# State-space loop of a decoder layer: every fourth product of state and C moves from VectorE to GpSimd, reading an SBUF copy of C

## The chip, the cores and the metric

One core of a Trainium2 chip. The metric is the device time of one execution in microseconds (us), and lower is better.

The core has five engines with an instruction queue each: TensorE (PE in the profile; its weight loads are PEld), VectorE (DVE), ScalarE (ACT), GpSimd (POOL) and SyncE (SP). Each runs its own instructions in the order of the program and waits on semaphores for the others. SBUF is the large on-chip memory, PSUM the small one that matmuls write; it has 8 banks of 512 float32 per partition. In this kernel GpSimd is given SBUF tiles alone.

## What is computed

The program is a small decoder of two layers on 1024 tokens of width 128. The change touches only its first part, a state-space block (`mamba`). Cut to what matters:

```python
dt, Bm, Cm = jnp.split(x_dbl, [DT_RANK, DT_RANK + D_STATE], axis=-1)
delta = softplus(dt @ dt_proj_w.T + dt_proj_b)        # 1024 x 256
A = -jnp.exp(A_log)                                   # 256 x 16
def step(s, inp):                                     # over the 1024 tokens
    d_t, B_t, C_t, u_t = inp
    dA = jnp.exp(d_t[..., None] * A)
    dBu = d_t[..., None] * B_t[:, None, :] * u_t[..., None]
    s = s * dA + dBu
    y = jnp.einsum('bds,bs->bd', s, C_t)
    return (s, y)
y = selective_scan(xi, delta, A, Bm, Cm, D)           # sum over 16 states, plus u * D
out = (y * silu(z)) @ out_proj_w.T + x
```

## The kernel before

Channels lie on the 128 partitions (two blocks of them, `c`), tokens on the free axis (1024 columns, two halves `q` of 512). The recurrence over tokens is one scan instruction for each half. So the work is a loop over 32 steps `n`: 2 blocks of channels times 16 states. A step does this:

- **B to SBUF.** TensorE spreads row `n % 16` of B over all partitions with two bf16 matmuls into PSUM banks 0 and 1 (`broadcast(…, 0, b_bcast)`, L386). ScalarE copies it to `b_all` (`copy_b`, L465), which has two slots. GpSimd multiplies it with `du` (delta times the input) into `drive` (L340), a ring of four.
- **Decay.** ScalarE computes exp(delta * A) for each half into PSUM banks 6 and 7 (`decay(n, q)`, L472). Bank 6 is rewritten once the first scan of the step before has read it, bank 7 once the second has.
- **Scan.** VectorE runs `scan(n, 0)` and `scan(n, 1)` (L293) into `state`, two slots; the second takes its initial value from the last column of the first.
- **Product with C.** TensorE spreads C's row over banks 2 and 3 (`broadcast(NS + n % NS, 2, c_bcast)`, the same line L386), and VectorE multiplies `state` with it into `read`, a ring of four (`read_out`, L301).
- **Sum.** TensorE adds `read` to banks 4 and 5 by matmuls with the identity in float32 (`add_state`, L395).

The order on each engine is written out by hand. VectorE: `scan(n, 0)`, `read_out(n-1)`, `scan(n, 1)`. ScalarE in step n: `decay(n, 0)`, `copy_b(n+1)`, `decay(n, 1)`. TensorE in step n: B of n+2 (after `copy_b(n+1)` has read the banks), C of n (after `read_out(n-1)` has read them), `add_state(n-1)`. After 16 steps `gated(0)` adds the skip term (L305) and multiplies by the gate `zs` (L309); `gated(1)` does the same at the end. The output projection and the rest of the layer follow the block.

In the words of the sections below, B(n), C(n) and add(n) are these groups of matmuls on TensorE.

Of the kernel before, what the change touches and what calls it, by code (L numbers as in the profile page):

```python
# [16 lines left out]
ALU = mybir.AluOpType  # L17
ACT = mybir.ActivationFunctionType
# [5 lines left out]
P = 128  # L24
S = 1024
# [4 lines left out]
HALF = 512  # L30
# [90 lines left out]
def mamba(nc, g, t, m):  # L121
# [3 lines left out]
    DI, NS, DR = 2 * D, 16, D // 16  # L125
    NC = DI // P
    TAPS = 4
    ps = g["psum"]
# [30 lines left out]
    du = relu  # L159
# [4 lines left out]
    b_all = m.sb("b_all", [P, 2, S])  # L164
    RING = 4
    drive = m.sb("drive", [P, RING, S])
    state = m.sb("state", [P, 2, S])
    read = m.sb("read", [P, RING, S])
    y = m.sb("y", [P, NC, S])

# [15 lines left out]
    var_ready, root_ready = m.sem("var_ready"), m.sem("root_ready")  # L186
    N_LOADS = 13
    STEPS = NC * NS
    DT0 = BC3

    def wide(b):
        return ps[:, b:b + 2, :].rearrange("p b n -> p (b n)")

    with nc.Block() as block:
        @block.sync
# [24 lines left out]
        def _(dve):  # L220
# [60 lines left out]

            def scan(n, q):
                dve.wait_ge(decay_ready, 2 * n + q + 1)
                if n >= 2:
                    dve.wait_ge(read_ready, n - 1)
                first = slice(q * HALF, (q + 1) * HALF)
                if q == 0:
                    dve.wait_ge(drive_ready, n + 1)
                    before = 0.0
                else:  # L290
                    dve.wait_ge(scanned, 2 * n + 1)
                    before = state[:, n % 2, HALF - 1:HALF]
                dve.tensor_tensor_scan(state[:, n % 2, first], ps[:, 6 + q, :], drive[:, n % RING, first], before,  # L293
                                       ALU.mult, ALU.add).then_inc(scanned, 1)

            def read_out(n):
                dve.wait_ge(scanned, 2 * n + 2)
                dve.wait_ge(c_bcast, n + 1)
                if n >= RING:
                    dve.wait_ge(summed, n - RING + 1)  # L300
                dve.tensor_tensor(read[:, n % RING, :], state[:, n % 2, :], wide(2), ALU.mult).then_inc(read_ready, 1)  # L301

            def gated(c):
                dve.wait_ge(summed, NS * (c + 1))
# [5 lines left out]

            for n in range(STEPS):
                scan(n, 0)
                if n >= 1:
                    read_out(n - 1)
                if n == NS + 1:
                    gated(0)
                scan(n, 1)
            read_out(STEPS - 1)
# [7 lines left out]
        @block.gpsimd  # L326
        def _(pool):
            link = chained(pool, chain["pool"])
            pool.wait_ge(loaded, 16 * N_LOADS)
            w = w_in[:, 0:P].unsqueeze(1).to_broadcast([P, TAPS, P])  # L330
            pool.tensor_tensor(w_tap[:], w, tap_rows[:], ALU.mult).then_inc(taps_ready, 1)
            pool.wait_ge(xn_ready, 1)
            pool.tensor_tensor(g["x"][:], g["x"][:], xn[:], ALU.add).then_inc(x_added, 1)
            for n in range(STEPS):
                c = n // NS
                pool.wait_ge(du_ready, c + 1)
                pool.wait_ge(b_copied, n + 1)
                if n >= RING:
                    pool.wait_ge(scanned, 2 * (n - RING + 1))
                pool.tensor_tensor(drive[:, n % RING, :], du[:, c, :], b_all[:, n % 2, :],  # L340
                                   ALU.mult).then_inc(drive_ready, 1)

        @block.tensor
        def _(pe):
            pe.wait_ge(loaded, 16 * N_LOADS)
            transpose_tiles(pe, h, g["ident"][:], ps, h_ready, hT_psum)
# [36 lines left out]
            def broadcast(row, banks, done):  # L383
                sel = onehot[:, row:row + 1].to_broadcast([BC3, P])
                for n in range(2):
                    last = pe.matmul(ps[:, banks + n, :], sel, split[:, n * HALF:(n + 1) * HALF],  # L386
                                     start=True, stop=True)
                last.then_inc(done, 1)

            def add_state(n):  # L390
                pe.wait_ge(read_ready, n + 1)
# [10 lines left out]
            pe.wait_ge(b_copied, 1)  # L402
            broadcast(1, 0, b_bcast)
            for n in range(STEPS):
                if n + 2 < STEPS:
                    pe.wait_ge(b_copied, n + 2)
                    broadcast((n + 2) % NS, 0, b_bcast)
                if n >= 1:
                    pe.wait_ge(read_ready, n)
                broadcast(NS + n % NS, 2, c_bcast)  # L410
                if n >= 1:
                    add_state(n - 1)
            add_state(STEPS - 1)
            pe.wait_ge(y_ready, NC)
            for i in range(NT):
                for c in range(NC):
# [6 lines left out]
        def _(act):  # L423
# [36 lines left out]

            def copy_b(n):
                act.wait_ge(b_bcast, n + 1)
                if n >= 2:
                    act.wait_ge(drive_ready, n - 1)
                act.activation(b_all[:, n % 2, :], wide(0), ACT.Copy).then_inc(b_copied, 1)  # L465
# [10 lines left out]
            act.wait_ge(relu_ready, NC)  # L476
            for n in range(STEPS):
                decay(n, 0)
                if n + 1 < STEPS:
                    copy_b(n + 1)  # L480
                decay(n, 1)
            act.wait_ge(z_ready, 2)
            act.activation(zs[:, 1, :], zs[:, 1, :], ACT.Silu).then_inc(z_ready, 1)

# [5 lines left out]
NS = 64  # L490
# [2617 lines left out]
```

## Time and profile before

| | |
|---|---|
| time, median of 3 runs | 1830.77 us (1829.9 to 1832.34) |
| the profiled execution: its own time | 1832.86 us |
| the profiled execution: span from first to last instruction | 1831.1 us |
| mean granted clock of TensorE | 0.882 of full speed |
| busy over the span: PE, PEld, DVE, ACT, POOL | 80%, 43%, 72%, 50%, 38% |
| first scan of the loop starts | 50.42 us |
| `gated(1)` ends | 170.61 us |

The state-space loop takes the stretch from about 50 to 171 us of the span; everything else of the program is the same before and after. The shares over the whole span say little about this stretch, so the rows are read from it alone. In a timeline row the first number is the start in the span, the second the duration; `x2` means two instructions merged in one row; the bracket is the time that the engine was idle before, and which instruction released it. Ends of matmuls are modelled, so for TensorE the starts are used.

### The profile page before, as it was taken

The page shows a single profiled execution, that of the slowest core. Times are in us where ns is not written, and L with a number is a line of the kernel's source. Part 1 is how long each engine was busy: PE and PEld are TensorE (multiplying, and loading weights), DVE is VectorE, ACT ScalarE, POOL GpSimd, SP SyncE. Part 2 cuts the span into 40 slices and gives each one's busy share as a digit, 9 for nine tenths or more (in the row PEclk, how much of TensorE's full clock was granted, in tenths as well). Part 3 has the DMA queues.
Part 4 walks back from the last instruction along what each step waited for, and adds up shares of the span by engine and source line. Part 5 has one row for each costly group of instructions (what it writes and reads, how often), then busy time and mean ns, then how long its engine had stood idle before and what let it go on. Part 6 is the DMA issues. An engine that isn't in the chain of part 4 may idle for free. (4 is left out here: it accounts for less than half of the span.)

```text
span 1831.1 us, 19912 instructions
## 1 busy us (share of the span) xinstructions
PE 1457.1 (80%) x6613; PEld 791.4 (43%) x6669; DVE 1319.4 (72%) x3065; ACT 923.9 (50%) x1447; POOL 691.3 (38%) x524
## 2 busy tenths in 40 slices
PE   5776999899985467887888878888857538999798
PEld 2223444355543312544555545555545324333365
DVE  5998568655156479899989999999857465767433
ACT  4654213656312204786777778777831104666321
POOL 0764212122000003888788888878820020000012
PEclk8899999999977768899899999989887757999899
DMA  5000110000057100000000000000020030000000
GB/s 138 1 1 3 46 58 16 0 1 1 0 126 144 47 14 1 1 1 1 1 1 1 1 1 1 1 1 1 1 83 11 15 78 1 1 1 1 1 0 12
DMA packets 30685, 37.21 MB, mean 20 GB/s; under 512 B 13859, under 2 KB 23812, under 8 KB 29448
## 3 DMA queue, kind: packets, MB, share of 16 engines
q1 hardware_dynamic: 29028, 24.03, 4.8%
q10 hardware_dynamic: 1544, 11.79, 3.2%
q8 instruction: 57, 0.93, 0.2%
q14 instruction: 56, 0.46, 0.1%
HBM read 29.57 MB, written 6.24 MB: 20 GB/s over the span
## 5 line engine op out<-in xcount | busy, mean ns | idle before, releaser
L1461 PE MATMUL psum<-film_ka,film_context_qa 97*128 97x512 bf16 (+1 forms) x832 | 343.2, 414 | 143.8 <-DVE search_and_weigh_kept L1656 63.6
L1833 ACT ACTIVATE search_and_weigh_e<-psum,search_and_weigh_bias 128x512 f32<-128x512 f32 (+1 forms) x416 | 267.9, 666 | 110.2 <-PE psum L1463 105.4
L1656 DVE MAX8 search_and_weigh_kept<-psum 128x8 f32<-128x171 f32 (+2 forms) x1216 | 317.3, 323 | 5.0 <-PE psum L1463 3.8
L1463 PE MATMUL psum<-film_kb,film_context_qb 128*128 128x512 bf16 (+1 forms) x777 | 319.1, 411 | 0.0
L1682 DVE SCALAR_TENSOR_TENSOR search_and_weigh_e<-psum,film_context_top,search_and_weigh_e 128x512 f32<-128x512 f32 (+1 forms) x283 | 200.8, 717 | 36.8 <-ACT search_and_weigh_e L1833 34.6
L1704 POOL TENSOR_TENSOR search_and_weigh_e<-search_and_weigh_e,search_and_weigh_keep 128x512 f32<-128x512 f32 (+1 forms) x133 | 150.4, 1131 | 167.3 <-ACT search_and_weigh_keep L1812 163.3
L1461 PEld LDWEIGHTS psum<-film_ka,film_context_qa 97*128 97x128 bf16 x832 | 92.2, 111 | 250.2 <-DVE search_and_weigh_e L1682 95.7
L1738 PEld LDWEIGHTS psum<-ctx_rows,search_and_weigh_mean_T 128*128 128x128 f32 (+1 forms) x816 | 132.3, 208 | 32.8 <-issue 6.0
L1708 POOL TENSOR_TENSOR search_and_weigh_mean<-search_and_weigh_e 128x512 f32<-128x512 f32 (+1 forms) x104 | 133.9, 1288 | 12.7 <-DVE search_and_weigh_e L1682 5.6
L1713 POOL TENSOR_TENSOR search_and_weigh_mean<-search_and_weigh_mean,search_and_weigh_e 128x512 f32<-128x512 f32 (+1 forms) x104 | 127.7, 1227 | 8.2
L1738 PE MATMUL psum<-ctx_rows,search_and_weigh_mean_T 128*128 128x96 f32 (+1 forms) x816 | 129.0, 284 | 0.9
L2912 POOL TENSOR_TENSOR residual<-residual,top_expert_kept 128x1024 f32<-128x1024 f32 x7 | 16.5, 2350 | 295.5 <-DVE top_expert_kept L2869 295.5
L2675 DVE TENSOR_REDUCE gqa_attend_low<-psum 128x1 f32<-128x128 f32 (+7 forms) x128 | 93.9, 754 | 43.4 <-PE psum L2594 41.0
L1712 POOL TENSOR_TENSOR search_and_weigh_e<-search_and_weigh_e 128x512 f32<-128x512 f32 (+1 forms) x91 | 111.6, 1227 | 7.1
L2712 ACT ACTIVATE gqa_attend_prob<-psum 128x512 f32<-128x512 f32 x192 | 84.9, 486 | 51.9 <-PE psum L2607 51.1
L1463 PEld LDWEIGHTS psum<-film_kb,film_context_qb 128*128 128x128 bf16 x832 | 88.5, 106 | 49.9 <-issue 17.4
L985 PE MATMUL psum<-cross_attention_prob,ctx_rows 128*97 128x512 f32 (+1 forms) x204 | 98.1, 603 | 4.6 <-ACT cross_attention_prob L1039 4.6
L340 POOL TENSOR_TENSOR mamba_drive<-mamba_relu,mamba_b_all 128x1024 f32<-128x1024 f32 x32 | 77.2, 2414 | 64.7 <-ACT mamba_b_all L465 31.4
L1039 ACT ACTIVATE cross_attention_prob<-psum 128x1024 f32<-128x1024 f32 (+1 forms) x51 | 51.8, 1019 | 97.1 <-PE psum L998 96.4
L998 PE MATMUL psum<-oss_attention_qc_shifted,ctx_T 97*128 97x512 f32 (+1 forms) x204 | 99.4, 611 | 0.8 <-ACT oss_attention_qc_shifted L1030 0.8
L1811 ACT ACTIVATE search_and_weigh_keep<-search_and_weigh_e,search_and_weigh_below 128x512 bf16<-128x512 f32 (+1 forms) x133 | 93.7, 705 | 0.5
L968 PE MATMUL psum<-ctx_T,cross_attention_qc 97*128 97x512 f32 (+1 forms) x208 | 87.3, 576 | 0.7 <-issue 0.7
(547 smaller groups left out, 2687.5 us busy)
## 6 DMA issues: line engine op xcount, KB each, us to landing
film_kb<-film_k_rows ACTq DMA_DIRECT2D x4, 1601.0 KB
film_ka<-film_k_rows ACTq DMA_DIRECT2D x3, 1601.0 KB
ctx_T<-in_ctx_T SPq DMA_DIRECT2D x1, 2401.5 KB
gqa_experts_w<-in_L_ffn_W SPq DMA_DIRECT2D x1, 2048.0 KB
film_convolve_back<-in_dft_back SPq DMA_DIRECT2D x1, 1728.0 KB, 12.9
film_k_rows<-cross_attention_film_hi SPq DMA_DIRECT2D x6, 256.0 KB, 2.0
film_k_rows<-cross_attention_film_mid SPq DMA_DIRECT2D x6, 256.0 KB, 2.0
film_k_rows<-cross_attention_film_low SPq DMA_DIRECT2D x6, 256.0 KB, 2.0
```

Source lines behind the costliest of these rows:

```text
L985: last = pe.matmul(ps[0:CA, 6 + n, :], ctx[0:rows, k, :], prob[0:rows, k % 3, n * HALF:(n + 1) * HALF], start=k == 0, stop=k == KT - 1)
L998: last = pe.matmul(ps[0:rows, 2 * (k % 2) + n, :], ctx_T[:, k * P:k * P + rows], qc_shifted[:, n * HALF:(n + 1) * HALF], start=True, stop= ...
L1461: pe.matmul(out, a["qa"][0:ROWS, h, rows], a["ka"][0:ROWS, h, c + b:c + b + cols], start=True, stop=False)
L1463: last = pe.matmul(out, a["qb"][:, h, rows], a["kb"][:, h, c + b:c + b + cols], start=False, stop=True)
L1656: last = dve.max(kept[:, h % 2, first + s, :], bank[:, lo:hi])
L1682: dve.scalar_tensor_tensor(out=w, in0=weigh_bank(n, h), scalar=a["top"][:, NH * i + h, TOP - 1:TOP], in1=w, op0=ALU.is_ge, op1=ALU.mult).t ...
L1704: link(pool.tensor_tensor(w[h], w[h], keep[:, k % KEEPS, 0:width], ALU.mult))
L1708: link(pool.tensor_tensor(out, w[0], w[1], ALU.add))
L1712: link(pool.tensor_tensor(w[2], w[2], w[3], ALU.add))
L1713: pool.tensor_tensor(out, out, w[2], ALU.add).then_inc(mean_ready, 1)
L1738: last = pe.matmul(ps[:, 7, 0:DC], mean_T[0:r, n % 2, b:b + P], ctx[0:r, (c + b) // P, 0:DC], start=c + b == 0, stop=c + b + r == S2)
L1833: act.activation(e[:, n % RING, sub, 0:PIECES[u][1]], ps[:, SEARCH_BANKS + q % WEIGH_BANKS, 0:PIECES[u][1]], ACT.Exp, bias=bias[:, i % 2, ...
```

## The change

- `read_out(n)` for n = 1, 5, 9, ..., 29 (8 of 32) is taken from VectorE. GpSimd computes it behind `drive(n+2)`, from `state` and `c_all`, a new SBUF tile that ScalarE fills by `copy_c(n)` behind `decay(n, 1)`.
- TensorE's C of the step after such a product waits for `copy_c` and not for the product.
- `state` gets three slots instead of two, `b_all` three.
- ScalarE copies B two steps ahead: `copy_b(n+2)` stands between `decay(n, 0)` and `decay(n, 1)` where `copy_b(n+1)` stood. TensorE's B of n+2 still stands at the start of its step n, ahead of C of n.
- `add_state` runs two steps behind, and `gated(0)` one step later.

```diff
+    B_RING, STATES = 3, 3
+    b_all = m.sb("b_all", [P, B_RING, S])
+    c_all = m.sb("c_all", [P, S])
...
+    state = m.sb("state", [P, STATES, S])
...
+    POOL_EVERY, POOL_FIRST, POOL_LAG, ADD_LAG = 4, 1, 2, 2
...
+    def read_on_pool(n):
+        return n % POOL_EVERY == POOL_FIRST
...
             for n in range(STEPS):
                 scan(n, 0)
-                if n >= 1:
+                if n >= 1 and not read_on_pool(n - 1):
                     read_out(n - 1)
-                if n == NS + 1:
+                if n == NS + ADD_LAG:
                     gated(0)
                 scan(n, 1)
...
-                pool.tensor_tensor(drive[:, n % RING, :], du[:, c, :], b_all[:, n % 2, :],
+                pool.tensor_tensor(drive[:, n % RING, :], du[:, c, :], b_all[:, n % B_RING, :],
                                    ALU.mult).then_inc(drive_ready, 1)
+                r = n - POOL_LAG
+                if r >= 0 and read_on_pool(r):
+                    pool.wait_ge(scanned, 2 * r + 2)
+                    pool.wait_ge(c_copied, pool_reads(r + 1))
+                    if r >= RING:
+                        pool.wait_ge(summed, r - RING + 1)
+                    pool.tensor_tensor(read[:, r % RING, :], state[:, r % STATES, :], c_all[:],
+                                       ALU.mult).then_inc(pool_read, 1)
...
             for n in range(STEPS):
-                if n + 2 < STEPS:
-                    pe.wait_ge(b_copied, n + 2)
-                    broadcast((n + 2) % NS, 0, b_bcast)
+                if n == 0:
+                    broadcast(NS, 2, c_bcast)
+                if n + B_RING - 1 < STEPS:
+                    pe.wait_ge(b_copied, n + B_RING - 1)
+                    broadcast((n + B_RING - 1) % NS, 0, b_bcast)
                 if n >= 1:
-                    pe.wait_ge(read_ready, n)
-                broadcast(NS + n % NS, 2, c_bcast)
-                if n >= 1:
-                    add_state(n - 1)
-            add_state(STEPS - 1)
+                    if read_on_pool(n - 1):
+                        pe.wait_ge(c_copied, pool_reads(n))
+                    else:
+                        wait_read(pe, n - 1)
+                    broadcast(NS + n % NS, 2, c_bcast)
+                if n >= ADD_LAG:
+                    add_state(n - ADD_LAG)
+            for n in range(STEPS - ADD_LAG, STEPS):
+                add_state(n)
...
+            def copy_c(n):
+                act.wait_ge(c_bcast, n + 1)
+                if n >= POOL_EVERY:
+                    act.wait_ge(pool_read, pool_reads(n))
+                act.activation(c_all[:], wide(2), ACT.Copy).then_inc(c_copied, 1)
...
             for n in range(STEPS):
                 decay(n, 0)
-                if n + 1 < STEPS:
-                    copy_b(n + 1)
+                if n == 0:
+                    copy_b(1)
+                if n >= 1 and n + B_RING - 1 < STEPS:
+                    copy_b(n + B_RING - 1)
                 decay(n, 1)
+                if n == 0:
+                    copy_b(2)
+                if read_on_pool(n):
+                    copy_c(n)
```

How the queues stand. ScalarE from the loop's first copy on, before (L465 is `copy_b`, L472 `decay`):

```order
L465 ACTIVATE mamba_b_all<-psum 128x1024 [waits mamba_b_bcast]
L472 ACT_TABLE_LOAD [waits mamba_delta_ready]
L472 ACTIVATE psum<-mamba_delta,mamba_a_neg 128x512 [waits mamba_relu_ready]
L465 ACTIVATE mamba_b_all<-psum 128x1024 [waits mamba_b_bcast]
L472 ACTIVATE psum<-mamba_delta,mamba_a_neg 128x512 [waits mamba_delta_ready]
L472 ACTIVATE psum<-mamba_delta,mamba_a_neg 128x512 [waits mamba_scanned,mamba_delta_ready]
L465 ACTIVATE mamba_b_all<-psum 128x1024 [waits mamba_drive_ready,mamba_b_bcast]
```

The same place after (L496 is `copy_b`, L509 `decay`, L502 `copy_c`):

```order
L496 ACTIVATE mamba_b_all<-psum 128x1024 [waits mamba_b_bcast]
L509 ACT_TABLE_LOAD [waits mamba_delta_ready]
L509 ACTIVATE psum<-mamba_delta,mamba_a_neg 128x512 [waits mamba_relu_ready]
L496 ACTIVATE mamba_b_all<-psum 128x1024 [waits mamba_b_bcast]
L509 ACTIVATE psum<-mamba_delta,mamba_a_neg 128x512 [waits mamba_delta_ready]
L496 ACTIVATE mamba_b_all<-psum 128x1024 [waits mamba_b_bcast]
L509 ACTIVATE psum<-mamba_delta,mamba_a_neg 128x512 [waits mamba_scanned,mamba_delta_ready]
L496 ACTIVATE mamba_b_all<-psum 128x1024 [waits mamba_drive_ready,mamba_b_bcast]
L509 ACTIVATE psum<-mamba_delta,mamba_a_neg 128x512 [waits mamba_scanned,mamba_delta_ready]
L502 ACTIVATE mamba_c_all<-psum 128x1024 [waits mamba_c_bcast]
L509 ACTIVATE psum<-mamba_delta,mamba_a_neg 128x512 [waits mamba_scanned,mamba_delta_ready]
```

One more copy of B stands ahead of the first decay of step 1, so from there on the copy inside a step is B(n+2) and not B(n+1); and behind the second decay of step 1 stands the copy of C, with the first decay of step 2 behind it.

TensorE in steps 0 and 1, before (L386 with `mamba_b_copied` starts a B group, L386 with `mamba_read_ready` a C group, L395 is `add_state`):

```order
L386 MATMUL psum<-mamba_split,mamba_onehot 128x512 [waits mamba_b_copied]
L386 MATMUL psum<-mamba_split,mamba_onehot 128x512 x3
L386 MATMUL psum<-mamba_split,mamba_onehot 128x512 [waits mamba_b_copied]
L386 MATMUL psum<-mamba_split,mamba_onehot 128x512
L386 MATMUL psum<-mamba_split,mamba_onehot 128x512 [waits mamba_read_ready]
L386 MATMUL psum<-mamba_split,mamba_onehot 128x512
L395 MATMUL psum<-mamba_read,ident 128x512 [waits mamba_read_ready]
L395 MATMUL psum<-mamba_read,ident 128x512
```

TensorE in steps 1 and 2, after (L411 is `broadcast`, L420 `add_state`):

```order
L411 MATMUL psum<-mamba_split,mamba_onehot 128x512 [waits mamba_b_copied]
L411 MATMUL psum<-mamba_split,mamba_onehot 128x512
L411 MATMUL psum<-mamba_split,mamba_onehot 128x512 [waits mamba_read_ready]
L411 MATMUL psum<-mamba_split,mamba_onehot 128x512
L411 MATMUL psum<-mamba_split,mamba_onehot 128x512 [waits mamba_b_copied]
L411 MATMUL psum<-mamba_split,mamba_onehot 128x512
L411 MATMUL psum<-mamba_split,mamba_onehot 128x512 [waits mamba_c_copied]
L411 MATMUL psum<-mamba_split,mamba_onehot 128x512
L420 MATMUL psum<-mamba_read,ident 128x512 [waits mamba_read_ready]
L420 MATMUL psum<-mamba_read,ident 128x512
```

The first sum stands one step later; the order inside a step is B, C, sum as before, and the C of step 2 waits for the copy of C in place of the product.

## Rows read from the trace of the kernel before

**Rows 1.** Busy time by stretch: us, then each engine's busy us (count), PEclk, DMA share.

```profile
64.00:109.00 45.00, 36.15 (x106) 13.99 (x105) 45.00 (x40) 30.34 (x40) 31.60 (x14) 1.00 0.00 1
...
117.40:124.30 6.90, 6.28 (x11) 2.58 (x12) 6.40 (x7) 3.50 (x6) 2.35 (x1) 0.53 0.00 0
```

**Rows 2.** Costliest groups, 64 to 109 us: count, busy us, mean ns, idle before, releaser.

```profile
L472 ACT ACTIVATE psum<-mamba_delta,mamba_a_neg 128x512 f32<-128x512 f32 x27 | 18.7, 692 | 14.6 <-DVE mamba_state L293 14.6
...
L386 PE MATMUL psum<-mamba_split,mamba_onehot 96*128 96x512 bf16 x52 | 15.6, 382 | 8.8 <-DVE mamba_read L301 8.8
```

**Rows 3.** Timeline, 98.8 to 105.8 us: start, duration, engine, line, operation, idle before.

```profile
98.92 1.19 DVE L301 TENSOR_TENSOR mamba_read<-mamba_state,psum 128x1024 f32<-128x1024 f32 x1
...
99.72 1.00 ACT L465 ACTIVATE mamba_b_all<-psum 128x1024 f32<-128x1024 f32 x1
100.04 1.27 DVE L293 TENSOR_TENSOR_SCAN mamba_state<-psum,mamba_state,mamba_drive 128x512 f32<-128x512 f32 x1
...
100.17 0.61 PE L386 MATMUL psum<-mamba_split,mamba_onehot 96*128 96x512 bf16 x2 [0.66 <-DVE mamba_read L301]
...
100.61 1.88 PE L395 MATMUL psum<-mamba_read,ident 128*128 128x512 f32 x4
...
101.23 1.19 DVE L293 TENSOR_TENSOR_SCAN mamba_state<-psum,mamba_drive 128x512 f32<-128x512 f32 x1
101.40 0.69 ACT L472 ACTIVATE psum<-mamba_delta,mamba_a_neg 128x512 f32<-128x512 f32 x1 [0.67 <-DVE mamba_state L293]
...
102.33 0.60 PE L386 MATMUL psum<-mamba_split,mamba_onehot 96*128 96x512 bf16 x2
...
102.51 0.69 ACT L472 ACTIVATE psum<-mamba_delta,mamba_a_neg 128x512 f32<-128x512 f32 x1 [0.42 <-DVE mamba_state L293]
103.14 1.00 ACT L465 ACTIVATE mamba_b_all<-psum 128x1024 f32<-128x1024 f32 x1
103.46 1.27 DVE L293 TENSOR_TENSOR_SCAN mamba_state<-psum,mamba_state,mamba_drive 128x512 f32<-128x512 f32 x1
```

**Rows 4.** Timeline, 44 to 64 us: the first steps of the loop.

```profile
50.42 1.21 DVE L293 TENSOR_TENSOR_SCAN mamba_state<-psum,mamba_drive 128x512 f32<-128x512 f32 x1
...
51.73 1.28 DVE L293 TENSOR_TENSOR_SCAN mamba_state<-psum,mamba_state,mamba_drive 128x512 f32<-128x512 f32 x1
52.35 1.00 ACT L465 ACTIVATE mamba_b_all<-psum 128x1024 f32<-128x1024 f32 x1
...
53.26 0.68 ACT L472 ACTIVATE psum<-mamba_delta,mamba_a_neg 128x512 f32<-128x512 f32 x1
...
54.05 1.20 DVE L301 TENSOR_TENSOR mamba_read<-mamba_state,psum 128x1024 f32<-128x1024 f32 x1
...
56.35 1.20 DVE L293 TENSOR_TENSOR_SCAN mamba_state<-psum,mamba_drive 128x512 f32<-128x512 f32 x1
```

**Rows 5.** Timeline, 44 to 64 us: a copy that waits for TensorE, and step 4's first scan.

```profile
61.88 1.03 PE L386 MATMUL psum<-mamba_split,mamba_onehot 96*128 96x512 bf16 x4
...
62.52 1.02 ACT L465 ACTIVATE mamba_b_all<-psum 128x1024 f32<-128x1024 f32 x1 [0.37 <-PE psum L386]
...
63.58 1.22 DVE L293 TENSOR_TENSOR_SCAN mamba_state<-psum,mamba_drive 128x512 f32<-128x512 f32 x1 [0.30 <-POOL mamba_drive L340]
```

**Rows 6.** Timeline, 100 to 120 us: a GpSimd product and a VectorE product of SBUF tiles.

```profile
111.11 2.34 POOL L340 TENSOR_TENSOR mamba_drive<-mamba_relu,mamba_b_all 128x1024 f32<-128x1024 f32 x1 [1.07 <-ACT mamba_b_all L465]
111.59 2.95 DVE L309 TENSOR_TENSOR mamba_y<-mamba_y,mamba_zs 128x1024 f32<-128x1024 f32 x1
```

**Rows 7.** Timeline, 100 to 120 us: TensorE after a pause.

```profile
118.02 1.03 PE L386 MATMUL psum<-mamba_split,mamba_onehot 96*128 96x512 bf16 x2 [3.92 <-DVE mamba_read L301]
```

**Rows 8.** Timeline, 150 to 180 us: the end of the loop.

```profile
161.23 1.19 DVE L293 TENSOR_TENSOR_SCAN mamba_state<-psum,mamba_drive 128x512 f32<-128x512 f32 x1
...
164.04 3.99 PE L395 MATMUL psum<-mamba_read,ident 128*128 128x512 f32 x8
...
169.38 1.23 DVE L309 TENSOR_TENSOR mamba_y<-mamba_y,mamba_zs 128x1024 f32<-128x1024 f32 x1
```

More of the change, by code:

```diff
@@ L163, in mamba @@
     split = m.sb("split", [BC3, S], BF16)
-    b_all = m.sb("b_all", [P, 2, S])
+    B_RING, STATES = 3, 3
+    b_all = m.sb("b_all", [P, B_RING, S])
+    c_all = m.sb("c_all", [P, S])
     RING = 4
     drive = m.sb("drive", [P, RING, S])
-    state = m.sb("state", [P, 2, S])
+    state = m.sb("state", [P, STATES, S])
     read = m.sb("read", [P, RING, S])
@@ L186, in mamba @@
     var_ready, root_ready = m.sem("var_ready"), m.sem("root_ready")
+    c_copied, pool_read = m.sem("c_copied"), m.sem("pool_read")
     N_LOADS = 13
     STEPS = NC * NS
+    POOL_EVERY, POOL_FIRST, POOL_LAG, ADD_LAG = 4, 1, 2, 2
     DT0 = BC3
@@ L192, in wide, with pool_reads, wait_read @@
         return ps[:, b:b + 2, :].rearrange("p b n -> p (b n)")
+    def read_on_pool(n):
+        return n % POOL_EVERY == POOL_FIRST
+    def pool_reads(n):
+        return sum(read_on_pool(k) for k in range(n))
+    def wait_read(eng, n):
+        if read_on_pool(n):
+            eng.wait_ge(pool_read, pool_reads(n + 1))
+        else:
+            eng.wait_ge(read_ready, n + 1 - pool_reads(n + 1))
     with nc.Block() as block:
@@ L283, in scan @@
                 dve.wait_ge(decay_ready, 2 * n + q + 1)
-                if n >= 2:
-                    dve.wait_ge(read_ready, n - 1)
+                if n >= STATES:
+                    wait_read(dve, n - STATES)
                 first = slice(q * HALF, (q + 1) * HALF)
@@ L291, in scan @@
                     dve.wait_ge(scanned, 2 * n + 1)
-                    before = state[:, n % 2, HALF - 1:HALF]
-                dve.tensor_tensor_scan(state[:, n % 2, first], ps[:, 6 + q, :], drive[:, n % RING, first], before,
+                    before = state[:, n % STATES, HALF - 1:HALF]
+                dve.tensor_tensor_scan(state[:, n % STATES, first], ps[:, 6 + q, :], drive[:, n % RING, first], before,
                                        ALU.mult, ALU.add).then_inc(scanned, 1)
@@ L300, in read_out @@
                     dve.wait_ge(summed, n - RING + 1)
-                dve.tensor_tensor(read[:, n % RING, :], state[:, n % 2, :], wide(2), ALU.mult).then_inc(read_ready, 1)
+                dve.tensor_tensor(read[:, n % RING, :], state[:, n % STATES, :], wide(2), ALU.mult).then_inc(read_ready, 1)
             def gated(c):
@@ L390, in add_state @@
             def add_state(n):
-                pe.wait_ge(read_ready, n + 1)
+                wait_read(pe, n)
                 if n == NS:
@@ L404, in _ @@
             for n in range(STEPS):
-                if n + 2 < STEPS:
-                    pe.wait_ge(b_copied, n + 2)
-                    broadcast((n + 2) % NS, 0, b_bcast)
-                if n >= 1:
-                    pe.wait_ge(read_ready, n)
-                broadcast(NS + n % NS, 2, c_bcast)
-                if n >= 1:
-                    add_state(n - 1)
-            add_state(STEPS - 1)
+                if n == 0:
[3 more added lines that the diff above has]
+                    broadcast((n + B_RING - 1) % NS, 0, b_bcast)
+                if n >= 1:
+                    if read_on_pool(n - 1):
+                        pe.wait_ge(c_copied, pool_reads(n))
+                    else:
+                        wait_read(pe, n - 1)
[4 more added lines that the diff above has]
+                add_state(n)
             pe.wait_ge(y_ready, NC)
@@ L462, in copy_b @@
                 act.wait_ge(b_bcast, n + 1)
-                if n >= 2:
-                    act.wait_ge(drive_ready, n - 1)
-                act.activation(b_all[:, n % 2, :], wide(0), ACT.Copy).then_inc(b_copied, 1)
+                if n >= B_RING:
+                    act.wait_ge(drive_ready, n - B_RING + 1)
+                act.activation(b_all[:, n % B_RING, :], wide(0), ACT.Copy).then_inc(b_copied, 1)
+            def copy_c(n):
[3 more added lines that the diff above has]
+                act.activation(c_all[:], wide(2), ACT.Copy).then_inc(c_copied, 1)
             def decay(n, q):
@@ L478, in _ @@
                 decay(n, 0)
-                if n + 1 < STEPS:
-                    copy_b(n + 1)
+                if n == 0:
+                    copy_b(1)
+                if n >= 1 and n + B_RING - 1 < STEPS:
+                    copy_b(n + B_RING - 1)
                 decay(n, 1)
+                if n == 0:
+                    copy_b(2)
+                if read_on_pool(n):
+                    copy_c(n)
             act.wait_ge(z_ready, 2)
```

## The prediction

> **What bounds the loop now.** I read the stretch of the loop first, because the shares of the whole span say nothing about it. From 64 to 109 us VectorE is busy for 45.00 of 45.00 us, TensorE for 36.15, GpSimd for 31.60, ScalarE for 30.34 [rows 1]. So VectorE's own instructions set the pace. Then the groups: ScalarE's decays were released by VectorE's scans, and TensorE's C waited for VectorE's product [rows 2]. Nobody makes VectorE wait in the steady part. Last the timeline of one step [rows 3]. The reader is to see `scan(15, 0)` at 101.23, the product behind it, `scan(15, 1)` at 103.46; the same second scan of step 14 stands at 100.04. One step takes 3.42 us.
>
> The same rows hold what the change leans on. I name them by step. The product of step 13 ends at 98.92 + 1.19 = 100.11. That releases C(14) at 100.17, then add(13) at 100.61, then B(17) at 102.33. ScalarE runs the first decay of step 16 at 102.51 and `copy_b(17)` at 103.14. A copy can start 0.64 us after its B has started (61.88 to 62.52, where the copy did wait) [rows 5], so B(17) is ready at 102.97. It is 0.17 us early. **The margin between TensorE and ScalarE is 0.17 us of a step of 3.42**, and the whole-span shares hide it.
>
> **The product that goes away.** Between the starts of the two scans of a step lie 2.23 us with a product (101.23 to 103.46) [rows 3] and 1.31 us without one, where the second scan has to wait for the first (50.42 to 51.73) [rows 4]. Eight products less are worth 8 x 0.92 = 7.4 us, if VectorE stays the bound. The Trainium skill (VectorE: DVE Perf Modes, section "The DRAIN you can't avoid") says that a semaphore between VectorE instructions costs nothing extra. By that rule the distance would be 1.12 us and the gain 9.0 us; the trace does not agree, its row shows 1.31 us, so I keep 7.4.
>
> **GpSimd** takes 2.34 us for such a product [rows 6]. Four drives and one product of state and C are 11.7 us in four steps, against 13.7 us that four steps take now. It fits, with less room, and nothing below needs a slower GpSimd.
>
> **The copy of B, one step further ahead.** This is the term that decides. In step 15 ScalarE now wants B(17), not B(16), between its two decays. But TensorE makes B(17) when it did before: at the head of its step 15, behind C(14) and the sum, so ready at 102.97 [rows 3, 5]. ScalarE would be free for it at 99.72 [rows 3]; it waits 3.2 us, and its second decay of step 15 is queued behind. A decay starts 0.91 us after a copy (52.35 to 53.26) [rows 4] and lasts 0.69. So it starts at 103.88 instead of 101.40 [rows 3] and ends at 104.57. `scan(15, 1)` starts there, about 0.06 us later (an estimate, from the 0.06 us between the product's end and C), at 104.63 instead of 103.46: 1.17 us late, on the path. Three slots of `b_all` do not help, since the PSUM banks of B are single and TensorE's order is unchanged. That the sum in front of B is now add(12) and not add(13) does not shorten it.
>
> Followed round, this is a closed loop: end of the product of step 13, +0.06 C(14), +2.16 B(17), +0.64 ready, +0.91 decay starts, +0.69 it ends, +0.06 `scan(15, 1)`, +1.19 `scan(16, 0)`, +1.11 product of step 15 (2.23 less the 1.12 from 98.92 to 100.04), +1.19 its end [rows 3]. The sum is 8.01 us, and the product of step 15 releases C(16) and so on. It spans two steps: **4.00 us a step instead of 3.42**. Every second product is in this chain, the even or the odd ones. The products given to GpSimd are 1, 5, 9, ..., all odd; the chain of the even ones holds none of them. So taking them away does not shorten it, and the 7.4 us are not seen.
>
> **The copy of C** stands ahead of the first decay of the next step. Where TensorE is slow at the start it is the late one: product of step 0 ends at 55.25, C(1) needs 1.03 us at that clock (the length of such a pair at half speed) [rows 4, 7], the copy 0.93, the decay 0.69, so `scan(2, 0)` starts near 58.0 instead of 56.35 [rows 4]. I carry +1.6 us from it to step 4. Later it sits inside the 8 us pattern and adds nothing.
>
> **The sum.** From the first scan of step 4 to that of step 31 are 27 steps: 161.23 - 63.58 = 97.65 us now [rows 5, 8], the pause at `gated(0)` included; 27 x 4.00 = 108.0 after, so +10.4. `gated(0)`: its second instruction multiplies two SBUF tiles; with a GpSimd product from 111.11 to 113.45 beside it, it took 2.95 us and ended 1.09 us after that product, and 1.23 us when GpSimd was idle [rows 6, 8]. It can again wait out a GpSimd instruction. Its two instructions, the first taken as long as the second when undisturbed, are 2.5 to 4.7 us, partly in the slack that VectorE now has; between 0 and 4.7 I take +1.8, as the pauses of VectorE around it are about as long as the rest. The Trainium skill (GPSIMD Engine Reference, section "Key points") has GpSimd contend with VectorE instructions of two SBUF inputs; by it, as by the rows, the scans and the products with PSUM pay nothing, and the sum stays. Tail: C(31), then three sums instead of two behind the product of step 30, 1.72 us each (100.61 to 102.33) [rows 3], less the wait that the last one had: +1.3. Start +1.6. Together 10.4 + 1.8 + 1.6 + 1.3 = **+15.1 us with TensorE at full speed**.
>
> **The clock.** TensorE works 0.44 + 1.72 + 0.44 = 2.6 us a step [rows 3]: 76% of 3.42 us, 65% of 4.00, and less evenly. C behind a GpSimd product no longer waits for VectorE, its work bunches, and a gap of about 2.8 us follows once in four steps. After an idle 3.9 us the row at 118.02 shows the half-speed length [rows 7], and from 117.40 to 124.30 the granted clock was 0.53, that is mostly the lower level of 1.2 GHz [rows 1]. Such a dip doubles the 2.16 us from C to B and stretches the rest, some +2.6 us on one turn of the loop. From none to one in each four steps is 0 to 8 dips, 0 to 21 us. I take one or two, +4 us, since the gap is shorter than the one seen. That makes +19.
>
> The profiled execution took 1832.9 us, so about 1852; against the median of the runs, which is 2 us lower, 1850.
>
> **Rivals.**
> - *Faster, by the saved products* (8%). If ScalarE found B in time in spite of the order, VectorE stays the bound: 1830.8 - 7.4 = 1823. It needs B(17) at 101.8 or earlier: `scan(15, 1)` at 103.46 less the 0.06, 0.69 and 0.91. It comes at 102.97, so 1.2 us of my chain would have to be wrong. For it speaks only that matmul ends are modelled; the copy at 62.52 that waited is against it.
> - *Only the copy of C costs* (8%). In a step with `copy_c` it starts after C, 0.64 us behind the product's end, and the first decay of the next step behind it: `scan(n+1, 0)` some 1.3 us late and the next scan 0.4, less 0.92 gained. 8 x 0.8 = +6: 1837. It holds if the wait for B were not there.
> - *No change* (4%): the two above cancel, within 0.2%, 1827 to 1834.
> - *The clock stays low in the loop* (10%). Then TensorE's 2.6 us become 5.2 a step and bind for long parts. Twelve such steps at 1.2 us more than 4.00 on top of the sum: about +29, 1860.
>
> **How the numbers follow.** My forecast has 70%: 1850, own range 1843 to 1858 (no dip: 1846; four dips: 1856). For 8 in 10 I take in part of the rivals on both sides: 1839 to 1861. Slower by over 0.2% (3.7 us, about what a measurement of this kernel can tell): 0.70 + 0.08 + 0.10 = 0.88. Same 0.04, faster 0.08.
>
> **What would show it.** Right, if in the steady part two steps take 8.0 us; if ScalarE's `copy_b` (L496) waits for TensorE (L411) some 3 us in every second step and is the longest wait of ScalarE in the loop; if VectorE is idle about 1.2 us in front of second scans, released by the decay (L509); if the GpSimd products take 2.3 to 2.4 us; and if the loop ends near 186 to 191 us instead of 170.6. The clock row of the loop shows whether there were dips. Wrong, if steps take 3.2 us and VectorE is still busy without a gap, or if VectorE waits for GpSimd.

## The result: 1.6% slower, and the profile after

The changed kernel took 1858.85 us (median of 4 runs, 1856.92 to 1859.15) against 1830.34 us before. The ratio is 1.0156, with a 95% interval of 1.0142 to 1.0171. The profiled execution took 1856.92 us, its span is 1855.1 us. The forecast was 1850, with 1839 to 1861 for 8 in 10.

Where the 24 us between the two profiled executions (1856.92 and 1832.86) lie is soon told. The end of `gated(1)` moved from 170.61 to 196.75 us, and the first instruction of the next part of the program (its batch norm statistics on VectorE) from 177.2 to 201.7 us. From there to the end of the span it is 1653.9 us before and 1653.5 after. The loop has the whole loss, and a little more: the output projection between the two gave 1.6 us back (4.9 us instead of 6.6; before, the granted clock was at the lower level from 171.7 to 175.1 us, after, it was not).

First the busy time by stretch of the changed kernel, in the columns of [rows 1]:

```profile
64.00:109.00 45.00, 31.88 (x82) 12.29 (x81) 34.39 (x30) 25.67 (x34) 30.92 (x14) 0.90 0.00 1
...
79.80:83.20 3.40, 3.40 (x6) 1.08 (x5) 2.56 (x3) 0.00 (x0) 1.01 (x1) 0.54 0.00 0
83.20:90.10 6.90, 4.24 (x14) 1.74 (x12) 4.70 (x4) 4.58 (x6) 4.70 (x2) 0.97 0.00 0
```

VectorE, which was busy for 45.00 of 45 us [rows 1], is busy for 34.39. It is not the bound any more, and neither is any other engine: GpSimd has 30.92, TensorE 31.88. The granted clock of the stretch is 0.90 instead of 1.00; the two rows below it show one dip (79.80 to 83.20 us at 0.54, that is the lower level of 1.2 GHz for nearly all of it) and the recovery behind it. Of such dips of 3.4 us the loop has eight by the granted clock; before, it had one pause with 6.9 us at 0.53 [rows 1].

Then the waits of the whole loop (46 to 200 us): who waited for whom, us in total, times, the longest.

```profile
...
ACT mamba_b_all L496 <- PE psum L411: 48.4, 28, 4.9
PE psum L411 <- DVE mamba_read L318: 40.0, 19, 3.8
DVE mamba_state L310 <- ACT psum L509: 33.4, 22, 2.8
...
ACT mamba_c_all L502 <- PE psum L411: 10.4, 7, 2.4
```

The first line is the one that the prediction asked for: ScalarE's `copy_b` waits for TensorE. The third is its price: VectorE's scans wait for decays. The kernel before has 5.0 us of the first pair in its whole loop and nothing of the second; there ScalarE's decays waited for VectorE [rows 2].

Last the timeline, three places of it: steps 8 and 9 with a dip of the clock, steps 11 to 13 without one, and `gated(0)`.

```profile
79.00 0.61 PE L411 MATMUL psum<-mamba_split,mamba_onehot 96*128 96x512 bf16 x2 [2.66 <-DVE mamba_read L318]
...
79.44 3.56 PE L420 MATMUL psum<-mamba_read,ident 128*128 128x512 f32 x4
...
82.80 1.08 PE L411 MATMUL psum<-mamba_split,mamba_onehot 96*128 96x512 bf16 x4
...
83.49 1.02 ACT L496 ACTIVATE mamba_b_all<-psum 128x1024 f32<-128x1024 f32 x1 [4.87 <-PE psum L411]
...
85.13 1.28 DVE L310 TENSOR_TENSOR_SCAN mamba_state<-psum,mamba_state,mamba_drive 128x512 f32<-128x512 f32 x1 [2.77 <-ACT psum L509]
...
95.88 1.20 DVE L310 TENSOR_TENSOR_SCAN mamba_state<-psum,mamba_drive 128x512 f32<-128x512 f32 x1
...
98.25 0.61 PE L411 MATMUL psum<-mamba_split,mamba_onehot 96*128 96x512 bf16 x2 [2.52 <-DVE mamba_read L318]
...
98.69 1.88 PE L420 MATMUL psum<-mamba_read,ident 128*128 128x512 f32 x4
...
99.31 1.20 DVE L310 TENSOR_TENSOR_SCAN mamba_state<-psum,mamba_drive 128x512 f32<-128x512 f32 x1
...
100.41 0.60 PE L411 MATMUL psum<-mamba_split,mamba_onehot 96*128 96x512 bf16 x2
...
101.05 1.02 ACT L496 ACTIVATE mamba_b_all<-psum 128x1024 f32<-128x1024 f32 x1 [3.07 <-PE psum L411]
...
101.97 1.29 ACT L509 ACTIVATE psum<-mamba_delta,mamba_a_neg 128x512 f32<-128x512 f32 x2
...
102.69 1.28 DVE L310 TENSOR_TENSOR_SCAN mamba_state<-psum,mamba_state,mamba_drive 128x512 f32<-128x512 f32 x1 [1.07 <-ACT psum L509]
...
103.88 1.20 DVE L310 TENSOR_TENSOR_SCAN mamba_state<-psum,mamba_drive 128x512 f32<-128x512 f32 x1
...
129.57 2.35 POOL L357 TENSOR_TENSOR mamba_drive<-mamba_relu,mamba_b_all 128x1024 f32<-128x1024 f32 x1
130.17 2.83 DVE L326 TENSOR_TENSOR mamba_y<-mamba_y,mamba_zs 128x1024 f32<-128x1024 f32 x1
```

Steps 11 to 13 are to be held against [rows 3]. C follows the product at 98.25, the sum at 98.69, B at 100.41, so B comes 2.16 us behind C as before. But the copy at 101.05 has now waited 3.07 us for it, the two decays stand behind it, and the second scan at 102.69 comes after 1.07 us in which VectorE had nothing to do. From the first scan of step 11 (95.88) to that of step 13 (103.88) are 8.00 us, at full clock, in the changed kernel itself. In the dip the sum takes 3.56 us instead of 1.88, B starts 3.80 us behind C, and the scan at 85.13 has waited 2.77 us.

### The profile page after: what moved, and what is told of

It reads as the page before. It is cut to its first block and busy times, and to the rows that moved or that the text cites. A ratio compares the mean times of both kernels' runs of the same rounds, so it can differ in the third digit from the quotient of the medians.

```text
span 1855.1 us, 19926 instructions
## 1 busy us (share of the span) xinstructions
PE 1461.2 (79%) x6613; PEld 789.5 (43%) x6669; DVE 1312.8 (71%) x3057; ACT 928.9 (50%) x1455; POOL 709.6 (38%) x532
## 3 DMA queue, kind: packets, MB, share of 16 engines
q10 hardware_dynamic: 1544, 11.79, 3.1%
```

## The experiments

Eight kernels. For the verdicts I use the end of `gated(1)` in the profiled execution, which shows the loop alone, and then the time. The loop begins between 49.5 and 51.2 us in these ten executions, so a difference of under 2 us in its end means little by itself; the third column leaves the start out. Four steps in a row at full clock are the cleanest measure of all. Each kernel has one profiled execution; the ratios are against executions of the kernel before taken beside it.

| kernel | `gated(1)` ends, us | loop's first scan to that end, us | four steps at full clock, us | median time, us | ratio to before (95%) |
|---|---|---|---|---|---|
| before | 170.61 | 120.2 | 13.7 | 1830 to 1834 | 1 |
| changed | 196.75 | 146.7 | none without a dip (two steps: 8.00) | 1858.85 | 1.0156 (1.0142 to 1.0171) |
| changed, all products on VectorE | 193.7 | 143.0 | 16.0 | 1854.80 | 1.0126 (1.0091 to 1.0162) |
| before, copy of B two ahead | 193.4 | 142.2 | 16.0 | 1852.88 | 1.0135 (1.0101 to 1.0169) |
| changed, B three ahead | 175.6 | 125.6 | 14.2 | 1843.60 | 1.0072 (1.0050 to 1.0094) |
| changed, filler matmuls | 188.5 | 137.8 | 16.0 | 1848.10 | 1.0097 (1.0065 to 1.0129) |
| changed, B three ahead, no GpSimd product | 170.0 | 120.0 | 13.7 | 1831.64 | 0.9995 (0.9979 to 1.0011) |
| changed, copy of B one ahead | 189.8 | 139.5 | 16.2 | 1854.77 | 1.0110 (1.0084 to 1.0135) |
| changed, B three ahead, copy of C moved | 161.3 | 111.8 | 12.8 | 1825.20 | 0.9963 (0.9947 to 0.9978) |
| the same, sums one behind | 161.0 | 110.9 | 12.8 | 1828.03 | 0.9962 (0.9945 to 0.9978) |

**All products on VectorE.** The edit, on the changed kernel:

```diff
     def read_on_pool(n):
-        return n % POOL_EVERY == POOL_FIRST
+        return False
```

> The changed kernel with all 32 products of state and C on VectorE and no copy of C. Theory A (ScalarE's copy of B is wanted one step earlier than TensorE delivers it; the even products carry the loop of 8.0 us for two steps): nothing is gained back. Two steps at full clock stay at 8.0 us, ScalarE still waits some 3 us for B in every second step, and the time is 20 to 30 us above the kernel before (ratio 1.011 to 1.016), 1850 to 1860. Rival B (the GpSimd products or the copies of C are what costs): the loss goes, 1828 to 1835, steps of 3.42 us.

Measured: 1854.80 us, loop end at 193.7. Neither the GpSimd products nor the copies of C cause the loss; without them it is 3 us smaller, with five dips of the clock instead of eight. Four steps without a dip (155.59 to 171.60 us) are 16.0 us. Theory A stands, rival B falls.

**The one edit by itself**, on the kernel before:

```diff
-    b_all = m.sb("b_all", [P, 2, S])
+    b_all = m.sb("b_all", [P, 3, S])
...
             for n in range(STEPS):
                 decay(n, 0)
-                if n + 1 < STEPS:
-                    copy_b(n + 1)
+                if n == 0:
+                    copy_b(1)
+                if n >= 1 and n + 2 < STEPS:
+                    copy_b(n + 2)
                 decay(n, 1)
+                if n == 0:
+                    copy_b(2)
```

> The kernel before with one edit of the change alone: b_all has three slots and ScalarE copies B(n+2) between the decays of step n. Theory A: this edit by itself makes the whole loss, +15 us at full clock and up to +28 with dips of the clock: 1846 to 1860; ScalarE waits for TensorE about 3.2 us in every second step. Rival B: no change, 1828 to 1833, since an earlier copy can only help when GpSimd, the lag of the sums or the third state buffer is what hurts.

Measured: 1852.88 us, loop end at 193.4: 22.8 of the 26.1 us come from asking for B one step earlier, nothing else changed; five dips of the clock are in them. Its waits, 46 to 200 us:

```profile
ACT mamba_b_all L465 <- PE psum L386: 62.8, 29, 5.7
...
DVE mamba_state L293 <- ACT psum L472: 23.1, 20, 3.6
```

and VectorE's timeline, the first scans of steps 24 and 28, where the clock was at its full level:

```profile
156.57 1.20 DVE L293 TENSOR_TENSOR_SCAN mamba_state<-psum,mamba_drive 128x512 f32<-128x512 f32 x1
...
172.57 1.20 DVE L293 TENSOR_TENSOR_SCAN mamba_state<-psum,mamba_drive 128x512 f32<-128x512 f32 x1
```

16.00 us for four steps: the 4.00 us a step of the prediction, to the hundredth.

**TensorE's B one step further ahead too**, on the changed kernel:

```diff
                 if n == 0:
                     broadcast(NS, 2, c_bcast)
-                if n + B_RING - 1 < STEPS:
-                    pe.wait_ge(b_copied, n + B_RING - 1)
-                    broadcast((n + B_RING - 1) % NS, 0, b_bcast)
+                    pe.wait_ge(b_copied, 2)
+                    broadcast(2, 0, b_bcast)
+                if n + B_RING < STEPS:
+                    pe.wait_ge(b_copied, n + B_RING)
+                    broadcast((n + B_RING) % NS, 0, b_bcast)
```

> The changed kernel with TensorE's B also one step further ahead: B(n+3) at the head of step n, ScalarE's copy unchanged. Theory A: the wait of ScalarE for B goes, the steps without a copy of C run at 3.42 us or less, and what is left is the copy of C behind the second decay: by a step table with the durations of the trace some 3.5 to 3.6 us a step, end of the loop at 174 to 180 us instead of 196.8, so 1834 to 1841. Rival B: no better than the changed kernel, 1855 to 1860.

Measured: loop end at 175.6 us, inside the expectation; the time of 1843.60 us is 3 us above it. Four steps take 14.2 us. The wait for B is gone, and what is left shows in the timeline of step 9, whose product is GpSimd's, so that C has to be copied:

```profile
83.77 0.61 PE L411 MATMUL psum<-mamba_split,mamba_onehot 96*128 96x512 bf16 x2 [0.66 <-DVE mamba_read L318]
...
84.42 1.02 ACT L504 ACTIVATE mamba_c_all<-psum 128x1024 f32<-128x1024 f32 x1 [2.14 <-PE psum L411]
...
85.33 0.69 ACT L511 ACTIVATE psum<-mamba_delta,mamba_a_neg 128x512 f32<-128x512 f32 x1
...
86.06 1.22 DVE L310 TENSOR_TENSOR_SCAN mamba_state<-psum,mamba_drive 128x512 f32<-128x512 f32 x1 [1.15 <-ACT psum L511]
```

C at 83.77, its copy at 84.42 after ScalarE has waited 2.14 us for it, the first decay of the next step queued behind at 85.33, and the scan 1.15 us late. This is the second flaw of the change: four steps are 0.5 us longer than before (14.2 to 13.7), though one product is saved in them. The time is further above before (13 us) than the loop is (5 us); this is taken up at the end.

**Filler for the clock**, on the changed kernel. It adds matmuls with zero weights to the running sum, so no value changes (`none` is the tile of zeros):

```diff
+    none = m.sb("none", [BC3, P], BF16)
+    FILL = 3
...
+                if n > ADD_LAG and n != NS + ADD_LAG:
+                    for _ in range(FILL):
+                        pe.matmul(ps[:, 4, :], none[:], split[:, 0:HALF], start=False, stop=False)
                 if n >= 1:
                     if read_on_pool(n - 1):
```

> The changed kernel, and in each step from 3 on (but step 18) three more matmuls on TensorE, in front of C, with weights of zero added to the running sum: 0.65 us of work that changes no value, put where TensorE is idle. It tells the term of the clock from the term of the order. Theory A with my split (15 us by the order at full clock, 11 by eight dips of the clock): the granted clock of the loop is 1.00 but for the start and perhaps one place, two steps take 8.0 to 8.2 us, loop ends at 184 to 190 us, 1844 to 1852. Rival C (the dips are the cause and the order costs little): back to 1830 to 1836. Rival D (the clock dips cost nothing, the order makes all of it): no change or slower, 1857 to 1865.

Measured: 1848.10 us, loop end at 188.5, 8.3 us earlier than the changed kernel, with 84 matmuls more. Busy time and clock, 64 to 129 us, and VectorE's first scans of steps 8, 12 and 16:

```profile
64.00:129.00 65.00, 52.77 (x171) 21.21 (x170) 53.86 (x45) 39.19 (x52) 47.27 (x21) 1.00 0.00 1
```

```profile
80.44 1.20 DVE L313 TENSOR_TENSOR_SCAN mamba_state<-psum,mamba_drive 128x512 f32<-128x512 f32 x1
...
96.44 1.20 DVE L313 TENSOR_TENSOR_SCAN mamba_state<-psum,mamba_drive 128x512 f32<-128x512 f32 x1
...
112.44 1.20 DVE L313 TENSOR_TENSOR_SCAN mamba_state<-psum,mamba_drive 128x512 f32<-128x512 f32 x1
```

Steps 8 to 16 take 16.00 and 16.00 us at clock 1.00: the GpSimd products of these eight steps gain nothing, as forecast. The pause at `gated(0)` kept one dip of 6.8 us. So the loss has two parts, the order (what is left here, 17.9 us with that dip) and the dips that the order brings about (8 us and more). Rivals C and D both fall.

**B three ahead, no GpSimd product:** the two edits above together.

> The changed kernel with TensorE's B(n+3) at the head of step n and with all products on VectorE, no copy of C. Theory A: VectorE sets the pace again, four steps take 13.7 us, gated(1) ends at 170 to 172 us, the time is that of the kernel before within 0.3% but for what the later parts do. It shows that the order of B is all that the other edits cost. Rival B: something else of the change costs as well (the sums two steps behind, the third buffer), end of the loop later than 174 us.

Measured: 1831.64 us, ratio 0.9995, loop end at 170.0. VectorE from 64 to 109 us:

```profile
64.00:109.00 45.00, 37.58 (x110) 14.54 (x108) 45.00 (x40) 31.56 (x42) 32.75 (x14) 1.00 0.00 1
```

45.00 of 45 us, as in [rows 1]. With B made as early as it is asked for, the loss is gone. The sums two steps behind are not quite free: from the first scan of step 31 to the end are 10.69 us against 9.38 before, 1.3 more, and the same total comes out because the steps behind `gated(0)` were shorter (steps 20 to 24 took 13.68 us against 14.79). Of the rest of the change, the third state buffer among it, no cost shows.

**The copy of B one ahead again**, on the changed kernel, with the GpSimd products kept:

```diff
-                if n == 0:
-                    copy_b(1)
-                if n >= 1 and n + B_RING - 1 < STEPS:
-                    copy_b(n + B_RING - 1)
+                if n + 1 < STEPS:
+                    copy_b(n + 1)
                 decay(n, 1)
-                if n == 0:
-                    copy_b(2)
```

> The changed kernel with the copy of B again one step ahead (copy_b(n+1) between the decays of step n), all else as changed: GpSimd products, copy of C behind the second decay, sums two steps behind. It tells what the copy of C costs where the wait for B is gone. My prediction's rival had +6 us for it (1837). The step table, which now follows TensorE's queue too, says more: C waits for the copy, B behind it is late, 4.0 to 4.1 us a step at full clock, gated(1) ends at 187 to 195 us, 1846 to 1856. If the copy of C costs only its own 0.8 us each, gated(1) ends near 176 us.

Measured: 1854.77 us, loop end at 189.8, four steps 16.2 us. The loop lost 19 us, where the prediction's second rival had +6 for the case without the wait for B. Its timeline at a GpSimd step:

```profile
88.73 1.02 ACT L502 ACTIVATE mamba_c_all<-psum 128x1024 f32<-128x1024 f32 x1 [2.14 <-PE psum L411]
...
90.26 1.01 ACT L496 ACTIVATE mamba_b_all<-psum 128x1024 f32<-128x1024 f32 x1
...
91.41 2.36 POOL L357 TENSOR_TENSOR mamba_drive<-mamba_relu,mamba_b_all 128x1024 f32<-128x1024 f32 x1 [3.36 <-PE psum L420]
...
93.72 2.35 POOL L365 TENSOR_TENSOR mamba_read<-mamba_state,mamba_c_all 128x1024 f32<-128x1024 f32 x1
93.90 1.23 DVE L310 TENSOR_TENSOR_SCAN mamba_state<-psum,mamba_drive 128x512 f32<-128x512 f32 x1 [0.73 <-POOL mamba_drive L357]
```

The copy of C pushes the decay, and with it the copy of B (90.26) and GpSimd's drive (91.41; the bracket names TensorE's sum, but the copy of B had just ended, at 91.27). The GpSimd product comes on top at 93.72, and VectorE waits for GpSimd. So with the copy of C where the change put it, asking for B one step later brings little back. Whether the GpSimd products need B two steps ahead at all is not shown: no kernel here has the copy of B one ahead and the copy of C moved.

**Both repairs.** On the kernel with B three ahead, the copy of C goes between the copy of B and the second decay of the next step:

```diff
                     copy_b(n + B_RING - 1)
+                if n >= 1 and read_on_pool(n - 1):
+                    copy_c(n - 1)
                 decay(n, 1)
                 if n == 0:
                     copy_b(2)
-                if read_on_pool(n):
-                    copy_c(n)
```

> The changed kernel with two edits: TensorE's B(n+3) at the head of step n, and the copy of C not behind the second decay of its step but behind the copy of B of the next step, so that the first decay no longer waits for it. Theory A, by a step table with the durations of the trace: GpSimd's products give their gain now, 3.2 us a step, gated(1) ends at 161 to 165 us against 170.6 before and 175.6 with the first edit alone; VectorE busy for over 97% of 64 to 109 us; some 6 to 9 us below the kernel before, if the later parts stay as they are: 1821 to 1827. Rival B (GpSimd's products cannot pay at this rate, by contention or by the extra copy): not below 1830, and VectorE waits for GpSimd or for a decay.

Measured: 1825.20 us, ratio 0.9963 (0.9947 to 0.9978), faster than before. The loop ends at 161.3 us, 9.3 us earlier. Busy time from 64 to 107 us, then the timeline from the first scan of step 8 to that of step 12:

```profile
64.00:107.00 43.00, 36.93 (x111) 14.98 (x110) 42.60 (x39) 34.16 (x45) 39.05 (x17) 1.00 0.00 1
```

```profile
74.49 1.20 DVE L310 TENSOR_TENSOR_SCAN mamba_state<-psum,mamba_drive 128x512 f32<-128x512 f32 x1
...
79.02 0.60 PE L411 MATMUL psum<-mamba_split,mamba_onehot 96*128 96x512 bf16 x2
...
79.83 1.00 ACT L498 ACTIVATE mamba_b_all<-psum 128x1024 f32<-128x1024 f32 x1
...
80.28 0.61 PE L411 MATMUL psum<-mamba_split,mamba_onehot 96*128 96x512 bf16 x2 [0.66 <-DVE mamba_read L318]
...
80.92 1.02 ACT L504 ACTIVATE mamba_c_all<-psum 128x1024 f32<-128x1024 f32 x1
...
81.33 1.19 DVE L310 TENSOR_TENSOR_SCAN mamba_state<-psum,mamba_drive 128x512 f32<-128x512 f32 x1
...
82.66 1.28 DVE L310 TENSOR_TENSOR_SCAN mamba_state<-psum,mamba_state,mamba_drive 128x512 f32<-128x512 f32 x1
...
87.28 1.20 DVE L310 TENSOR_TENSOR_SCAN mamba_state<-psum,mamba_drive 128x512 f32<-128x512 f32 x1
```

VectorE is busy for 42.60 of 43 us, and GpSimd for 39.05. Four steps take 12.79 us (74.49 to 87.28) against 13.69 before. The copy of C at 80.92 ends while the scan runs, and the decay behind it starts at 81.84, in time for the scan at 82.66. B, begun at 79.02 and so ready 0.64 us later [rows 5], at 79.66, is copied at 79.83: the 0.17 us of the kernel before are back, no more, since both ends have moved by one step.

**The same with sums one step behind** (`ADD_LAG` 1 instead of 2).

> As the kernel with both edits, and the sums one step behind as in the kernel before. Theory A: the steady steps are the same, the tail is one sum shorter: gated(1) ends 0 to 2 us earlier than with the sums two steps behind, at 160 to 164 us. Rival: a sum one step behind has to wait for the GpSimd product in TensorE's queue and holds up B and C behind it: 165 to 172 us.

Measured: loop end at 161.0 us, ratio 0.9962: no different in time from the one before it. The tail is shorter as expected, 9.37 us from the first scan of step 31 instead of 10.70, and 0.9 us of it is left over the whole loop (110.9 against 111.8 us); this one started 0.6 us later. Sums one step behind held nothing up.

## Why the prediction was right, and where it was off

- **The bound now, and the margin of 0.17 us:** right. It was the whole case. With B asked for one step earlier, ScalarE waited 3.07 us (3.2 forecast) and the scan came 1.07 us late (1.17 forecast).
- **The loop of 8.01 us for two steps:** right. It is 8.00 us in the changed kernel, and 16.0 us for four steps in the three kernels that keep this order of B (all products on VectorE, the one edit by itself, the filler).
- **The saved products are not seen:** right at full clock. With and without them the four steps take 16.0 us. Once B was early and the copy of C out of the way, they gave 0.90 us in each four steps (13.69 to 12.79), as the forecast 0.92 said for one product. Two scans without a product between them start 1.33 us apart there (81.33 to 82.66), near the 1.31 of [rows 4] and not the 1.12 that the prediction worked out by the Trainium skill (VectorE: DVE Perf Modes, section "The DRAIN you can't avoid"). What that section measures is eight copies with and without a semaphore behind each; it has no price for a scan that waits for the scan right in front of it, so the 1.12 was more than the section says.
- **GpSimd fits:** right; 2346 ns for a product, and 39.05 of 43 us busy in the fast kernel without VectorE waiting.
- **The copy of C:** at the start the +1.6 us came out in part by luck. Step 4 begins 15.21 us behind step 0 instead of 13.16, which is 2.05 more, and the loop happened to begin 0.41 us earlier. "Later it adds nothing" holds in the changed kernel. The rival built on it had +6 us if the wait for B were not there. With B made earlier the loop lost 5.0 us, near that size (the time 13 us, for which see the next section); with the copy of B one ahead it lost 19. There I had priced the late decay, and not that the copy of B and the drive stand behind it.
- **`gated(0)`:** its second instruction took 2.83 us, next to a GpSimd instruction that ran from 129.57; with the first's 1.25 us that is 4.1, inside the forecast 2.5 to 4.7. The pause cost 3.0 us instead of 1.8: the step with it takes 6.37 us, in the changed kernel and in the one with the filler, against 3.35 for a step of the same kind without it. **Tail:** +1.3 forecast, 10.70 instead of 9.38 us from the first scan of step 31, so +1.3.
- **The clock was the mis-sized term.** I took one or two dips at 2.6 us, +4 us. There were eight, all between step 4 and step 31. Held step by step against the kernel with the filler, seven of them cost 1.5 to 1.7 us each, 11.2 together (steps 12 to 16 take 17.7 us with one, steps 8 to 12 19.2 us with two, against 16.0). The eighth, from 181.9 us on, cost nothing: steps 28 to 31 take 11.79 us with it and 11.78 with the filler and no dip. The 2.6 us stood for a doubled way from C to B and more; at 79.00 that way took 3.80 us instead of 2.16, so 1.6 more and not 2.2, as C had begun before the clock fell.
- **The reason given for the dips was wrong too.** I put the gap in front of C down to the GpSimd products and took it as too short to lower the clock. But the two kernels without a GpSimd product in the late order of B have the same gaps, up to 2.66 us, and five dips each; so most of them come with the order, and the GpSimd products can have to do with three at most. The gap does not decide alone: the fall at about 79.5 us stands behind an idle 2.66 us, while behind the idle 2.52 us before 98.25 the clock stayed at its full level. What decides in the single case stays open.
- **The sum as measured:** from the first scan of step 4 to that of step 31 120.83 us instead of 97.66, which is +23.2: 10.4 by the order, 3.0 by the pause, 11.2 by seven dips, less 1.2 because steps 4 to 8 took 14.8 us and not 16, less 0.2 in the last three. With 1.6 at the start and 1.3 at the tail that is 26.1, what the loop lost.
- **The side:** the chance of 0.88 for slower was on the right side. The time lies inside the range for 8 in 10, but 0.85 us outside the forecast's own range of 1843 to 1858, and inside the wider one only since that took in part of the rivals. The likeliest value was 9 us low: the loop lost 7 more than the 19 forecast, by the dips; what stands behind the loop gave 2 back; and 4 came from going from profiled executions to medians, the one of the changed kernel being 2 us below its median and the one of the kernel before 2 above.

## The parts behind the loop

The edit touches nothing behind the loop, and yet the stretch from the next part's first instruction to the end of the span differs between profiled executions: 1647.5 us (before with the copy of B two ahead), 1653.0 to 1656.6 in seven of them, 1660.0 (changed, B three ahead) and 1660.6 (sums one behind). The time that TensorE's clock records show at the lower level in that stretch goes with it: 383.0 us in the first, 389.8 to 396.5 in the seven, 406.9 and 403.5 in the last two. One reading is that with another end of the loop the later bursts of TensorE fall otherwise against the changes of the clock. It is not tested, and the end of the loop can't be all: executions of one and the same kernel before lie between 1825.7 and 1836.3 us, and there too the shorter ones have the higher granted clock (0.886 against 0.881 at the two ends). In the kernel with B three ahead it was no chance of one execution, its five lie between 1842.6 and 1844.6 us: 13 us above before, with a loop only 5 us longer. It is why I took the end of the loop for the verdicts.

## What to carry to other kernels

Before an instruction is moved ahead in one queue, follow what it consumes into the other engines' queues, down to the single margin: here 0.17 us, on engines that were busy for 67% and 80% of the time. A deeper ring on the consumer's side brought nothing while the producer made the value in the same place (193.4 us); with both ends moved by one step the loss was gone (170.0 us). And give work to an idle engine only with its feeding copy placed where the instruction queued behind it is not made late: with B early, the copy of C behind the second decay cost 0.5 us in four steps, and in front of it the products gave 0.9.

## What the runs showed of the hardware that I had not expected

- TensorE's granted clock fell to its lower level eight times in the loop, for 3.4 us each; from 64 to 109 us TensorE was busy for 31.88 of 45 us. The first fall, at about 79.5 us, came behind an idle time of only 2.66 us, the one in the row at 79.00. With 0.65 us of filler a step (38.71 of 45 us busy) there was no fall between 64 and 129 us, and the loop ended 8.3 us earlier. Useless work made the kernel some 10 us faster.
- A product of two SBUF tiles on VectorE again waited out a GpSimd instruction: 130.17 to 133.00, beside 129.57 to 131.92, so it ended 1.08 us behind it, as before (1.09) [rows 6]. The traces have more of it than these two. In nine of the ten, a GpSimd instruction ran as this product began, and in all nine it ended 1.08 us behind that instruction, whether that made it 1.56 or 2.95 us long; in the tenth (sums one behind) GpSimd was idle, and it took 1.23 us. It goes the other way too: in three of them GpSimd's next instruction began while the product ran, and took 3.3 us instead of 2.35. The scans and the products with PSUM kept their durations beside a busier GpSimd (scans 1.20 and 1.28 us, products 1.20). The Trainium skill (GPSIMD Engine Reference, section "Key points") says the same of which instructions contend, and the traces agree.
